# Largest magnitude over the feed-forward channels: one strided reduction over four channel tiles in place of ScalarE's absolute values and two folds

## The reference

```python
def act_quant(x):
    scale = 127.0 / jnp.clip(jnp.max(jnp.abs(x), axis=-1, keepdims=True), 1e-05)
    return jnp.clip(jnp.round(x * scale), -128, 127) / scale
...
h = bit_linear(x, w1)                    # 256 -> 1024
h = depthwise_conv1d(h.transpose(0, 2, 1), conv_w, conv_b)
h = h.transpose(0, 2, 1)
h = jax.nn.silu(h)
return bit_linear(h, w2)                 # quantizes h per token, 1024 -> 256
```

## Time and profile before

| what | value |
|---|---|
| time, median of 3 runs | 399.28 us (397.93 to 400.9) |
| span of the profiled execution, first to last instruction | 397.3 us |
| TensorE busy | 364.4 us (92%) |
| VectorE busy | 306.3 us (77%) |
| ScalarE busy | 256.9 us (65%) |
| GpSimd busy | 215.4 us (54%) |
| mean granted TensorE clock | 0.990 |

### The profile page before, as it was taken

One profiled execution on the slowest core, in us unless ns is written; L12 is line 12 of the kernel. 1 busy time (PEld: TensorE's weight loads), 2 busy tenths in 40 slices (PEclk: granted clock), 3 DMA queues, 4 the chain that ended last, 5 costly groups with the idle time before them and its releaser, 6 DMA issues.

```text
span 397.3 us, 8398 instructions
## 1 busy us (share of the span) xinstructions
PE 364.4 (92%) x3029; PEld 272.9 (69%) x3029; DVE 306.3 (77%) x647; ACT 256.9 (65%) x483; POOL 215.4 (54%) x245
## 2 busy tenths in 40 slices
PE   6599799999999999999989999999999998987885
PEld 2277557877877796678767876787678776843733
DVE  2247659654599889888998698959895997799795
ACT  3213436668786779567868686768677966772552
POOL 5406689689379919892789427972993016000000
PEclk9989999999999999999999999999999999999999
DMA  8781521201100022002000220022012001000101
GB/s 238 167 183 32 167 86 29 54 10 27 26 12 2 2 53 48 19 20 55 18 0 2 60 45 2 2 61 42 12 26 51 19 2 34 4 2 0 35 2 35
DMA packets 21907, 16.71 MB, mean 42 GB/s; under 512 B 12435, under 2 KB 20936, under 8 KB 21865
## 3 DMA queue, kind: packets, MB, share of 16 engines
q1 hardware_dynamic: 20970, 15.11, 15.4%
q10 hardware_dynamic: 895, 1.06, 1.0%
HBM read 9.82 MB, written 3.38 MB: 33 GB/s over the span
## 4 chain that ended last, share of the span: by engine, by line
PE 69%; DVE 14%; ACT 7%; issue 5%; DMA 4%; SPq 1%; DVEq 0%; ACTq 0%
PE bank L1790 8%; PE bank L1870 8%; PE bank L1841 7%; PE bank L1884 6%; PE bank L1943 5%; PE bank L1913 4%; PE bank L1984 4%; PE bank L1944 4%; DMA shared<-in_x 4%; PE bank L1861 4%; PE bank L1737 3%; PE bank L1904 2%; ACT shared L1339 2%; PE bank L1803 2%; PE bank L1893 2%
## 5 line engine op out<-in xcount | busy, mean ns | idle before, releaser
L1502 DVE TENSOR_REDUCE mx<-bank 120x4 fp32r<-120x376 f32 (+3 forms) x88 | 44.0, 506 | 24.5 <-PE bank L1853 24.1
L1274 ACT COPY pT<-bank 94x480 f32<-94x480 f32 (+3 forms) x88 | 48.2, 554 | 21.0 <-PE bank L1870 20.7
L1266 ACT ACTIVATE pr<-bank 120x376 f32<-120x376 f32 (+3 forms) x88 | 39.6, 454 | 28.9 <-PE bank L1861 28.1
L1870 PE MATMUL bank<-cst,pr 120*94 120x120 f32 (+3 forms) x352 | 51.3, 271 | 2.7 <-ACT pr L1266 2.7
L1841 PE MATMUL bank<-kbd,q_hl 128*120 128x376 f32 (+3 forms) x176 | 51.1, 373 | 1.2 <-ACT pT L1274 0.6
L1114 POOL TENSOR_TENSOR rs<-ve,half_neg 110x3 f32<-110x3 f32 x16 | 16.7, 1045 | 63.9 <-DVE ve L1530 47.7
L1943 PE MATMUL bank<-xT_hi,w1T 128*128 128x330 f32 x128 | 44.2, 351 | 1.3 <-DVE late L1585 0.9
L1870 PEld LDWEIGHTS bank<-cst,pr 120*94 120x94 f32 (+3 forms) x352 | 36.1, 122 | 10.4 <-ACT pr L1266 6.4
L1121 POOL TENSOR_SCALAR xn<-h,mv,rs 110x256 f32<-110x256 f32 x21 | 27.6, 1323 | 24.7 <-PE bank L1778 24.4
L1136 POOL TENSOR_TENSOR rc<-qk,cst 110x320 f32<-110x320 f32 x22 | 20.0, 909 | 38.3 <-ACT qk L1237 37.4
L1944 PE MATMUL bank<-xT_lo,w1T 128*128 128x330 f32 x128 | 39.5, 314 | 0.0
(11 more groups left out here) (132 smaller groups left out, 882.6 us busy)
## 6 DMA issues: line engine op xcount, KB each, us to landing
kbd<-shared SPq DMA_DIRECT2D x56, 41.2 KB, 2.1
out<-h SPq DMA_DIRECT2D x7, 330.0 KB
wn<-in_w SPq DMA_DIRECT2D x2, 1024.0 KB, 6.7
shared<-in_x SPq DMA_DIRECT2D x4, 432.0 KB
h<-in_txt SPq DMA_DIRECT2D x1, 770.0 KB
late<-in_lin SPq DMA_DIRECT2D x1, 768.0 KB, 7.1
vw<-v_rows SPq DMA_DIRECT2D x8, 94.0 KB
v_rows<-qk SPq DMA_DIRECT2D x8, 82.5 KB
```

Of the source, the lines that this page charges most:

```text
L1266: nc.scalar.activation(pr[:, g % 3, 0:HKV * WIDTH[j]], S_BANKS[g % 2][0:QP, 0:HKV * WIDTH[j]], ACT.Exp, scale=HD ** -0.5).then_inc(exped, 1)
L1274: nc.scalar.copy(pT[0:WIDTH[j], g % 3, :], S_BANKS[g % 2][0:WIDTH[j], 0:HKV * QP]).then_inc(p_kept, 1)
L1502: nc.vector.tensor_reduce(mx[:, g % 4, :].bitcast(F32R), S_BANKS[g % 2][0:QP, 0:HKV * WIDTH[j]].rearrange("p (k c) -> p k c", k=HKV), axis ...
L1870: o = nc.tensor.transpose(S_BANKS[g % 2][0:w, kv * QP:(kv + 1) * QP], pr[:, g % 3, kv * w:(kv + 1) * w], ident[0:QP, 0:QP])
```

## The change

ScalarE's `abs_g` and VectorE's `fold_g` are gone, with their rows in the tables, their buffer `fold` and their semaphores. `max_g` is now, for each half, one `tensor_reduce` with maximum over four channel tiles and the absolute value applied to its input. It reads `us` with the tiles innermost: element (token t, tile m) lies 330 words behind (t, m - 1), and after the fourth tile it goes back to the next token. The last maximum of the two halves stays. `tanh` of the next pair now waits for `silued` in place of `folded`. No other tick is changed.

```diff
@@ act.abs_g and dve.fold_g leave the tables of ticks
-            "absed", "folded", "part_maxed", "g_maxed", ...
+             "part_maxed", "g_maxed", ...
...
                 act.wait_ge(conv_done, MH * n + HALFC * (p + 1))
                 if n:
-                    act.wait_ge(folded, NP * (n - 1) + p + 1)
+                    act.wait_ge(silued, NP * (n - 1) + p + 1)
                 nc.scalar.activation(th[:, ms, :], us[n % 2][:, ms, :], ACT.Tanh, scale=0.5).then_inc(tanhed, 1)
-
-            def abs_g(n, p):
-                ms = slice(HALFC * p, HALFC * (p + 1))
-                act.wait_ge(silued, NP * n + p + 1)
-                nc.scalar.activation(th[:, ms, :], us[n % 2][:, ms, :], ACT.Abs).then_inc(absed, 1)
...
-            def fold_g(n, p):
-
-                dve.wait_ge(absed, NP * n + p + 1)
-                if p:
-                    dve.wait_ge(part_maxed, NP * n + 1)
-                elif n:
-                    dve.wait_ge(g_maxed, n)
-                nc.vector.tensor_tensor(fold[:, :, :], th[:, HALFC * p:HALFC * p + 2, :], th[:, HALFC * p + 2:HALFC * (p + 1), :], ALU.max).then_inc(folded, 1)
-
             def max_g(n, p):
-                dve.wait_ge(folded, NP * n + p + 1)
+
+                ms = slice(HALFC * p, HALFC * (p + 1))
+                dve.wait_ge(silued, NP * n + p + 1)
                 if p == 0 and n:
                     dve.wait_ge(max_turned, n)
-                if p == 0:
-                    nc.vector.tensor_tensor(gm[:, 0, :], fold[:, 0, :], fold[:, 1, :], ALU.max).then_inc(part_maxed, 1)
-                else:
-                    nc.vector.tensor_tensor(gm[:, 1, :], fold[:, 0, :], fold[:, 1, :], ALU.max).then_inc(part_maxed, 1)
+                nc.vector.tensor_reduce(gm[:, p, :], us[n % 2][:, ms, :].rearrange("p m t -> p t m"), axis=AX.X, op=ALU.max,
+                                        apply_absolute_value=True).then_inc(part_maxed, 1)
+                if p:
                     dve.wait_ge(part_maxed, NP * (n + 1))
                     nc.vector.tensor_tensor(gm[:, 2, :], gm[:, 0, :], gm[:, 1, :], ALU.max).then_inc(g_maxed, 1)
```

More of the change, by code:

```diff
@@ L865, in build @@
         th, at = carve(wn, 0, 128, [MH, T])
-        fold, at = carve(wn, at, 128, [2, T])
         late = sb("late", [128, MH * D + KP * D])
@@ L968, in build @@
             "up_done", "mid_tap", "left_tap", "conv_done", "tanhed", "silued"))
-        absed, folded, part_maxed, g_maxed, max_turned, max2, clip2, scale2, undo2, diag_made = (sem(s) for s in (
-            "absed", "folded", "part_maxed", "g_maxed", "max_turned", "max2", "clip2", "scale2", "undo2", "diag_made"))
+        part_maxed, g_maxed, max_turned, max2, clip2, scale2, undo2, diag_made = (sem(s) for s in (
+             "part_maxed", "g_maxed", "max_turned", "max2", "clip2", "scale2", "undo2", "diag_made"))
         scale_spread, g_scaled, g_kept, down_done, ffn_added = (sem(s) for s in (
@@ L1350, in _ @@
             work = {name: due("act." + name) for name in (
-                "exp", "keep_xn", "keep_qk", "keep_q", "keep_ctx", "keep_sel", "quant_x", "high_x", "mid", "keep_p", "keep_k", "tanh", "abs_g", "conv_g", "keep_w", "sort_a", "keep_pix_a", "keep_patch")}
+                "exp", "keep_xn", "keep_qk", "keep_q", "keep_ctx", "keep_sel", "quant_x", "high_x", "mid", "keep_p", "keep_k", "tanh", "conv_g", "keep_w", "sort_a", "keep_pix_a", "keep_patch")}
             for q in TICKS:
@@ L1376, in _ @@
                     tanh(n, p)
-                for n, p in work["abs_g"].get(q, ()):
-                    abs_g(n, p)
                 for n, p in work["conv_g"].get(q, ()):
@@ L1652, in _ @@
             work = {name: due("dve." + name) for name in (
-                "max_s", "norm", "add_att", "stats1", "norm1", "rope", "keep_k", "var2", "norm2", "max_x", "quant_x", "low_x", "left", "right", "silu", "fold_g", "max_g", "scale2", "quant_g", "add_ffn", "sort_v", "keep_pix_v", "abs_w", "ternary")}
+                "max_s", "norm", "add_att", "stats1", "norm1", "rope", "keep_k", "var2", "norm2", "max_x", "quant_x", "low_x", "left", "right", "silu", "max_g", "scale2", "quant_g", "add_ffn", "sort_v", "keep_pix_v", "abs_w", "ternary")}
             for q in TICKS:
@@ L1684, in _ @@
                     silu(n, p)
-                for n, p in work["fold_g"].get(q, ()):
-                    fold_g(n, p)
                 for n, p in work["max_g"].get(q, ()):
```

20 lines of the change are left out of this document (removed).

## The result

The changed kernel takes 413.25 us (median of 4 runs, 412.55 to 416.37) against 399.62 us before: ratio 1.034, interval 1.030 to 1.038, 13.6 us slower. The forecast was 412.2 us. The profiled execution has a span of 412.1 us, 14.8 more than before.

What follows compares the result with a forecast made beforehand. TensorE was taken to bound pairs 0 to 5 and VectorE to lead in the last 47 us; 7.2 + 3.4 + 2.35 = +12.9 us on the median of 399.28 gave 412.2 us, range 399.5 to 417.5.

Steps and rivals of the forecast that it cites:

- The reduction's price: Each of 16 VectorE reductions of 1320 elements: 1.52 us at the lower end, 2.60 taken from L1407's copy.
- rival B: All reductions: the stride is free, each takes 1.52 us, whole 399.7 us, not slower; chance 0.22.
- Pairs 6 and 7: Last two pairs, no attention to cover VectorE: longer reductions add 3.36 us in pair 6 and 2.35 in pair 7.
- The lost cover ahead of the silu: Pair 6: the first fold ran free during the tanh wait; both reductions now follow the silu, 5.20 for 1.84 us.
- Pairs 0 to 5: 110 to 350 us: TensorE stalls behind VectorE's longer reductions; 7.2 us taken, between 0 and 14.4.
- the sum: Whole span: 7.2 + 3.4 + 2.35 = +12.9 us on 397.3, or 412.2 us on the median.
- the upper end: Pairs 0 to 5: TensorE stalls some 2.4 us in each of six pairs, 14.4 us.
- the other reason given: Pairs 0 to 5: VectorE's idle time, 33.5 us or 5.6 a pair, could let it catch up.
- Rival C: Behind pair 7's turn_max: TensorE's longer idling lowers its clock, 1.7 us more, 413.9 us; chance 0.08.
- D: VectorE reductions stretched by contention with GpSimd: 0.15 dearer, +2 us on the forecast, inside its range; no chance given.
- The signs named ahead: TensorE idle about 16 us to pair 5's end, VectorE busy 321, ScalarE 236, turn_max waits 3.4 and 2.35 longer.

Runs made afterwards that it cites:

- contig: Changed kernel with each reduction reading the same 1320 words in the order they lie, without the hop: 402.41 us, ratio 1.003 to the kernel before.
- new05: Kernel before with the changed maximum in pairs 0 to 5 alone: 408.74 us, ratio 1.021, +8.5 us.
- keepabs: Changed kernel with ScalarE's 16 absolute values put back, unread: 415.54 us, ratio 1.043 to the kernel before.
- fill2: Changed kernel with more TensorE filler products before the maximum's waits (29 for 13 in pair 6, 45 for 34 in pair 7): 412.89 us beside 413.09.

## Why the prediction was right

**The reduction's price** was bounded by 1.52 and 2.60 us, and 2.60 taken. It is 2.42. The kind of reason was right: L1407's spread writes were a better guide than ScalarE's strided read, which shows no price. contig measured the lower end, 1.52. The estimate of 2.4 from the Trainium skill ("Vector Engine (DVE) Microarchitecture Reference", section "Measured stream behaviour on trn2") was the closer one, and that section's single stream over two regions at full rate, which was named for rival B, was no guide to four tiles here.

**Pairs 6 and 7.** +3.36 and +2.35 forecast, +2.9 and +1.8 measured, and the difference is the price alone: the two reductions take 4.76 and 4.69 us there in place of 5.20, 0.4 and 0.5 us less. In pair 7, with the gap between them and the last maximum, 4.73 us stand for 2.89. The lost cover ahead of the silu is seen as the gap of 0.84 us.

**Pairs 0 to 5** were the guess of the sum: 7.2 us, the middle between 0 and 14.4. 8.7 in the profile, 8.5 by new05. The mechanism was the one forecast, TensorE stalled behind VectorE, and the upper end held: no pair adds more than 2.4 us in the steps listed above, and their mean is 1.6 where 1.2 was taken. In pair 0, whose rows gave the 2.46, the `shift` comes only 1.05 us later (126.62 for 125.57). A part of what was swallowed shows there, the exp and the tanh that no longer stand behind an absolute value on ScalarE. Tanh before and now:

```profile
117.76 1.30 ACT L1321 ACTIVATE wn<-shared 128x1320 f32<-128x1320 f32 x1
...
116.98 1.30 ACT L1300 ACTIVATE wn<-shared 128x1320 f32<-128x1320 f32 x1
```

So the place of the fold became a gap of 0.25 us there, and the second silu starts 0.8 us earlier, where the prediction had only a gap. Over all pairs the relief is some 2 us by keepabs, which is likely and not shown. Of the 5.7 us between the upper end and the 8.7, that leaves more than half to the other reason given, VectorE's own idle time, which no run sets apart. That the value is near the middle is luck: nothing in the trace of before chose it. The lower clock, which the prediction had only for pair 7, is not needed for it. In pair 4 of the profiled execution TensorE idled for 1.46 us up to 288.87 and was granted 0.76 and 0.67 in the next 6 us:

```profile
289.00:292.00 3.00, 3.00 (x28) 2.12 (x29) 3.00 (x3) 1.07 (x3) 1.33 (x3) 0.76 0.13 28
292.00:295.00 3.00, 3.00 (x22) 1.95 (x20) 2.08 (x9) 0.94 (x2) 0.88 (x1) 0.67 0.12 29
```

When the changed kernel ran again, its clock was 1.00 from 110 to 350 us, and the second silu of pair 6 came 9.1 us later than before, no earlier than in the profile with the fall.

**Rival C**, the clock behind the longer wait, had 0.08, and the fall came in the profile, in pair 6 as well, at 1.3 us for both (0.5 and 0.8) where 1.7 was forecast for one. Its size failed at the step that put all of TensorE's loss on the path: the 5 us behind pair 7's `turn_max` were granted 0.66, a third less, and the path lost 0.8 us. It should have had more than 0.08, with the waits of pairs 6 and 7 growing to over 3 us, as the prediction itself worked out. That the loss reaches the median isn't shown (fill2). Against the sum, the profile has 8.7 us for 7.2, 2.9 and 1.8 for 3.36 and 2.35, and 1.3 for the clock, which the sum had at nothing: errors of both signs, 14.8 in all for 12.9, and 13.6 in the medians. So the closeness of 413.3 to 412.2 is in part luck.

**Rival B** is refuted by the 2.42 us, and **D**, a stretching by GpSimd, by the spread of 2370 to 2472 ns. The signs named ahead came within their sizes: TensorE idle 15.7 us for "about 16", ScalarE 238 us busy for 236, waits before `turn_max` 2.9 and 1.8 us longer for 3.4 and 2.35. VectorE's 316.8 us fall short of 321: 2.9 us are the price, and the last maxima are 1.7 us shorter, which the prediction didn't see.

## What to carry to other kernels

Before merging folds into one strided reduction, count the words that it reads away from their neighbours: here a hop of 6 words or more at every element cost 0.69 us over a contiguous reduction for each 1000 elements, and the merge pays only where the folds and what they wait for cost more than that. A move behind a wait takes with it the cover that the wait gave, and the relief of an engine that bounds nothing buys little. Time the one instruction that has no row in the profile before the rest is planned: its duration decided this case.

## What was not expected of the hardware

A reduction step of 2 words ran at the full rate (1.52 us), and 6 words cost as much as 330 (2.49 and 2.42). A pass of one input and one output over 1320 uint32 words takes 0.83 us alone and had a mean of 1.1 us and up to 1.52 in pairs 0 to 4, with GpSimd at work beside it, so that three short contiguous instructions came out dearer (2.7 us a half) than one that reads each word alone (2.42). The silu, which has two inputs in SBUF and was not touched, took 1.91 to 2.18 us in three of its 16 executions in the changed kernel, each beside a step of GpSimd, and 2.02 in one of them before, where the others take about 1.53. That it meets GpSimd more often because the folds no longer do is a reading, and not shown.
